# GpSimd makes the first guesses of the reciprocal roots from block 2 on, and blocks 0 and 1 are started tile by tile with ScalarE's square roots

## The chip, the cores and the metric

The kernel runs on one core of one Trainium2 chip. The metric is the device time of that core in microseconds. Three runs of the kernel before took 392.67, 393.62 and 393.69 us; their median is 393.62 us.

## What is computed

The input x has 2 sequences of 4096 tokens with 256 features. Each token is layer-normalised; the result xn goes into two branches, and both are added to x.

```python
xn = (x - mean(x)) / sqrt(var(x) + 1e-5)
# branch 1: causal softmax pooling
h   = tanh(xn @ W1 + b1)                    # 256 -> 256
s   = h @ w2 + b2                           # one score a token
e   = exp(s - max over the sequence of s)
ctx = cumsum(e * xn) / cumsum(e)            # along the sequence
a   = tanh(concat(ctx, xn) @ Wc.T + bc)     # 512 -> 256
# branch 2: gated feed-forward, integer weights times 1/127
f   = (silu(xn @ wg.T) * (xn @ wu.T)) @ wd.T   # 256 -> 768 -> 256
out = x + a + f
```

## The kernel before

**Tiling.** The 8192 tokens are cut into 16 blocks of 512, a block into two pairs of 256 tokens, a pair into two tiles of 128. Matmuls take fp16 operands in two parts, a high part and the rest, so that one product is two or three passes. All sums are made in the 8 PSUM banks.

**Order.** The kernel is written as steps with a short name, a block and an index. Each engine's order is worked out while the program is built: `due_times()` gives every step a due time, `STEP` its engine, how long it keeps it and when its result is seen, `needs()` what it waits for, and the class `Plan` lets each engine take, at each modelled moment, the first step in order of due time that is ready and, if it opens a PSUM bank, finds one free. `SENT` and `X_SENT` are the modelled landings of the weights and of the first blocks of x. On the chip each engine then runs its own list in order and waits on semaphores.

**Steps around the change** (lines of the kernel before):

- `stats_first`, `root_first`, `normalise_first` (L958 to L1033), on VectorE, for block 0: statistics of four tiles, variance plus eps (L1014), ScalarE's square root (L1368), reciprocal and one Newton step, then four normalised tiles (L1031), signalled in pairs.
- Ahead of that TensorE runs `WARM` = 12 matmuls on constants (L1381), spreads the bias row b1 and the row w2 over the partitions by matmuls with ones (L1377), and runs twice `FILL` = 2 more matmuls on constants.
- `Lb` (L700): transposes of a normalised pair; `Xh` (L873, ScalarE) and `Xl` (L1091, VectorE): high part and rest of xn out of the bank. Only blocks 0 and 1 are turned like this; from block 2 on a pair is turned by transposing DMAs (`Tx`), after `Xh` (L869) and `Xm` (GpSimd, L1244).
- `W1h` (L917, ScalarE) and `W1l` (L1144, VectorE): the parts of W1. `Ea` (L912, ScalarE) copies the spread rows out of the last bank. `Ss` (L841, ScalarE) writes b1 into a bank before `S` (L707, TensorE) adds xn @ W1 to it; `Th` (L882, ScalarE) is its tanh, in place, and `Sv` (L1101, VectorE) the product with w2 and its sum. The bank is free after `Sv`.
- `Gg`, `Gu` (L743, TensorE, four 512-column matmuls each, 6 of either a block), `Sg` (L888, ScalarE, silu), `H` (L1116), `Hh` (L895), `Hl` (L1121), then `D` (L763, TensorE). `C` (L707 too) is the product with Wc.
- `Tb` (L914): ScalarE's load of the table with tanh and silu, after block 0's square root.
- `B` (L951, L955, VectorE): statistics of a pair. `R` (`root_seed`, L971, VectorE, four operations): first guess of the reciprocal root by an integer shift. `T` (`root_newton`, L985, GpSimd): three Newton steps and the shift, 14 small operations for a group of one or two blocks. `Ln` (L859, ScalarE) or `Lp` (L1239, GpSimd) normalises. `STAT_GROUPS` has ten groups; groups 1 to 9 go through `R` and `T`.
- `Wgh`, `Wuh`, `Wdh` (GpSimd, L1249, L1252, L1255): integer weights to fp16. `N` (L1225, L1230) and `Cl` (L1258): GpSimd's part of the context sums.
- The bank of an `Lb` is freed by `Xl`, and `S` of block 0 runs pair by pair.

Of the kernel before, what the change touches and what calls it, by code (L numbers as in the profile page):

```python
# [16 lines left out]
P = 128  # L17
# [10 lines left out]
EPS = 1e-5  # L28
# [16 lines left out]

STAT_GROUPS = [[0], [1], [2], [3], [4, 5], [6, 7], [8, 9], [10, 11], [12, 13], [14, 15]]
# [19 lines left out]
    "T": (PO, 1.35, 1.45), "N": (PO, 3.2, 3.3), "Cl": (PO, 1.2, 1.3), "Lp": (PO, 0.75, 0.85), "Xm": (PO, 1.5, 1.6),  # L66
# [3 lines left out]
    "Ea": (SE, 0.5, 0.63), "Tb": (SE, 1.4, 1.5), "W1h": (SE, 0.55, 0.7), "Wch": (SE, 1.06, 1.2), "Kx": (SE, 1.02, 1.2), "Ky": (SE, 1.02, 1.2),  # L70
    "W1l": (VE, 0.62, 0.75), "Wcl": (VE, 1.2, 1.3), "K1": (VE, 0.62, 0.75), "Kg": (VE, 0.9, 1.0), "Kh": (VE, 0.9, 1.0), "Ku": (VE, 0.5, 0.6), "Kd": (VE, 0.5, 0.6), "Ke": (VE, 0.5, 0.6),
    "Kc": (VE, 1.2, 1.3), "Kf": (VE, 0.75, 0.85), "Fl": (VE, 0.15, 0.25),
    "Wgh": (PO, 1.5, 1.6), "Wuh": (PO, 1.5, 1.6), "Wdh": (PO, 1.5, 1.6), "Kp": (TE, 0.15, 0.4),
# [3 lines left out]
OPENS = {"Kp": "Kp", "Lb": "Lb", "Ss": "S", "Gg": "Gg", "Gu": "Gu", "Cs": "C", "M1": "M1", "M2": "M2", "M3": "M3"}  # L77
CLOSES = {"Kp": "Fl", "Lb": "Xl", "S": "Sv", "Gg": "Sg", "Gu": "Hl", "D": "Da", "M1": "V1", "M2": "V2", "M3": "V3"}
# [55 lines left out]
def closing(group):  # L134
    kind, i, x = group
    if kind == "C":
        return ("Ct" if seeded(i, x) else "Ca"), i, x
    return CLOSES[kind], i, x


def closed_by(st):
    kind, i, x = st
    if kind in ("Ct", "Ca"):
        return ("C", i, x) if closing(("C", i, x)) == st else None
    for group, last in CLOSES.items():
        if last == kind:
            return group, i, x
    return None


def due_times():
# [26 lines left out]
    for g, blocks in enumerate(STAT_GROUPS):  # L178
        if g:
# [7 lines left out]
            due["R", g, 0] = root  # L187
            for n in range(NEWTON):
                due["T", g, n] = root + 0.1 + 1.4 * n
    for i in range(NBLK):  # L190
        for pr in range(2):
# [8 lines left out]
            due["Ss", i, pr] = due["S", i, pr] - (1.6 if i or not pr else 0.6)  # L200
            due["Th", i, pr], due["Sv", i, pr] = end["S", i, pr] + 0.1, end["S", i, pr] + 0.8
# [36 lines left out]
def needs(st, wide):  # L238
# [3 lines left out]
    if kind in ("W1h", "Wgh", "Ea"):  # L242
        return []
# [1207 lines left out]
```

## Time and profile before

| | us |
|---|---|
| runs of the kernel before | 392.67, 393.62, 393.69 |
| the profiled execution, its own time | 393.06 |
| its span on the core | 391.1 |
| TensorE busy in it | 385.9 |
| VectorE, ScalarE, GpSimd busy | 297.5, 235.6, 210.1 |

The span is what the views of the trace cover; 1.96 us of the execution lie around it. A start is in microseconds from the start of the span. PE is TensorE, PEld its weight loads, DVE VectorE, ACT ScalarE, POOL GpSimd, SP SyncE; L707 is line 707 of the kernel. A matmul's row gives when it starts and how long it takes through the array; matmuls are pipelined, so the distance of their starts is what they cost.

### The profile page before, as it was taken

The numbers are of one execution on the slowest core, as the hardware profiler recorded it, in microseconds if no ns is written. First come the engines' busy times: TensorE is split into PE (matmuls) and PEld (weight loads), VectorE is DVE, ScalarE is ACT, GpSimd is POOL, SyncE is SP. The second block draws the span as 40 slices with busy tenths as digits, with TensorE's granted clock in tenths as the row PEclk, the third lists the DMA queues.
The fourth block names the chain that finished last, engine by engine and source line by source line (L and its number), as shares of the span: only waits on it lengthen the run. The fifth ranks groups of instructions, "written<-read, shape, count | busy, mean of one in ns | idle before, by whom it ended". The sixth has DMA issues, their size and how long they took to land.

```text
span 391.1 us, 7885 instructions
## 1 busy us (share of the span) xinstructions
PE 385.9 (99%) x2740; PEld 268.7 (69%) x2740; DVE 297.5 (76%) x632; ACT 235.6 (60%) x434; POOL 210.1 (54%) x289
## 2 busy tenths in 40 slices
PE   8999999999999999999999999999999999999996
PEld 4556676757566686866877676767677676676765
DVE  6799998999996997876769966777676765754351
ACT  4766576689985659786556575364553644536250
POOL 1487586874629989794335405866456554502000
PEclk9999999999999999999999999999999999999999
DMA  8944525576834232475210005043231220100001
GB/s 275 348 158 69 137 53 134 106 189 89 201 72 96 54 83 81 116 165 97 76 34 29 27 28 164 28 128 87 58 72 55 90 85 26 54 28 28 28 28 61
DMA packets 54945, 36.56 MB, mean 93 GB/s; under 512 B 31858, under 2 KB 50292, under 8 KB 54900
## 3 DMA queue, kind: packets, MB, share of 16 engines
q1 hardware_dynamic: 54608, 35.73, 35.5%
q8 instruction: 24, 0.39, 0.4%
q10 hardware_dynamic: 292, 0.26, 0.2%
q14 instruction: 21, 0.17, 0.1%
HBM read 20.19 MB, written 8.45 MB: 73 GB/s over the span
## 4 chain that ended last, share of the span: by engine, by line
PE 97%; DVE 2%; issue 0%; DVEq 0%
PE bank L707 44%; PE bank L743 41%; PE bank L763 9%; PE bank L1381 1%; DVE ex L1121 0%; DVE stats L951 0%; PE bank L700 0%; PE bank L1377 0%; DVE veps L980 0%; DVE xt L1091 0%; DVE bank L1116 0%; DVE sg L1413 0%; PE bank L813 0%; DVE mv L955 0%; PE bank L819 0%
## 5 line engine op out<-in xcount | busy, mean ns | idle before, releaser
L743 PE MATMUL bank<-xt,narrow 128*128 128x512 f16 x768 | 177.3, 379 | 0.0
L743 PEld LDWEIGHTS bank<-xt,narrow 128*128 128x128 f16 x768 | 75.2, 98 | 75.4 <-DVE wide L1121 0.2
L707 PE MATMUL bank<-narrow,wide 128*128 128x256 f16 x792 | 96.4, 273 | 0.0
L707 PE MATMUL bank<-narrow,xt 128*128 128x256 f16 x768 | 92.8, 273 | 0.3 <-DVE xt L1091 0.3
L707 PEld LDWEIGHTS bank<-narrow,xt 128*128 128x128 f16 x768 | 75.0, 98 | 19.0 <-DVE xt L1091 0.6
L1258 POOL TENSOR_TENSOR wide<-ex,wide 128x512 f16<-128x512 f32 x32 | 39.4, 1248 | 87.6 <-ACT wide L909 87.6
L888 ACT ACTIVATE sg<-bank 128x512 f32<-128x512 f32 x96 | 57.2, 596 | 46.3 <-PE bank L743 45.6
L1116 DVE SCALAR_TENSOR_TENSOR bank<-bank,sg 128x512 f32<-128x512 f32 x96 | 66.1, 694 | 24.4 <-PE bank L743 21.3
L707 PEld LDWEIGHTS bank<-narrow,wide 128*128 128x128 f16 x792 | 77.5, 98 | 9.4
L895 ACT ACTIVATE wide<-bank 128x512 f16<-128x512 f32 x90 | 53.3, 596 | 47.7 <-DVE bank L1116 39.3
L1121 DVE TENSOR_TENSOR wide<-bank,wide 128x512 f16<-128x512 f32 x90 | 60.5, 678 | 9.9 <-ACT wide L895 8.6
L1139 DVE TENSOR_TENSOR_SCAN ex<-rows,ex 128x512 f32<-128x512 f32 x32 | 56.5, 1767 | 0.7 <-POOL ex L1230 0.7
L1230 POOL TENSOR_TENSOR ex<-ex,rows 128x512 f32<-128x512 f32 x32 | 44.8, 1401 | 9.2 <-DMA rows<-scratch 6.9
L1225 POOL TENSOR_TENSOR ex<-xt 128x512 f32<-128x512 f16 x32 | 44.6, 1395 | 0.2
L1125 DVE TENSOR_TENSOR xres<-bank,xres 128x512 f32<-128x512 f32 (+1 forms) x33 | 22.0, 667 | 26.4 <-PE bank L707 26.3
L841 ACT ACTIVATE bank<-every 128x512 f32<-128x512 f32 (+1 forms) x65 | 38.3, 594 | 0.0
L763 PE MATMUL bank<-narrow,wide 128*128 128x256 f16 x312 | 38.3, 273 | 0.0
L902 ACT ACTIVATE bank<-bank 128x512 f32<-128x512 f32 (+1 forms) x33 | 18.8, 569 | 31.0 <-PE bank L707 31.0
L763 PEld LDWEIGHTS bank<-narrow,wide 128*128 128x128 f16 x312 | 30.5, 98 | 7.4
L1130 DVE TENSOR_TENSOR xres<-bank,xres 128x512 f32<-128x512 f32 x28 | 19.3, 688 | 18.2 <-ACT bank L902 18.1
L1101 DVE CUSTOM_DVE_ANT_0 bank<-bank,every 128x256 f32<-128x256 f32 x64 | 25.4, 446 | 4.1 <-ACT bank L882 4.1
L1244 POOL TENSOR_TENSOR xt<-xnat,xt 128x512 f16<-128x512 f32 x14 | 16.9, 1226 | 11.3 <-ACT xt L869 11.3
(103 smaller groups left out, 262.3 us busy)
## 6 DMA issues: line engine op xcount, KB each, us to landing
rows<-scratch SPq DMA_DIRECT2D x16, 512.0 KB, 5.1
out_y<-xres SPq DMA_DIRECT2D x31, 256.0 KB, 2.1
xres<-in_x SPq DMA_DIRECT2D x15, 512.0 KB, 5.1
xt<-xt SPq DMA_TRANSPOSE x56, 2.5
wide<-in_wg SPq DMA_DIRECT2D x1, 768.0 KB, 5.9
wide<-in_wu SPq DMA_DIRECT2D x1, 768.0 KB, 8.4
wide<-in_wd SPq DMA_DIRECT2D x1, 768.0 KB, 10.1
wide<-in_wc SPq DMA_DIRECT2D x1, 512.0 KB, 11.1
```

Source lines behind the costliest of these rows:

```text
L707: return pe.matmul(dst, lhs, rhs, start=False, stop=stop, skip_group_check=True)
L743: mm = pe.matmul(b[:, :], pg.up(which, k, j), pg.xn(sx, k, tok), start=n == 0, stop=n == len(todo) - 1)
L763: mm = pe.matmul(dst, lhs, rhs, start=n == 0, stop=n == len(todo) - 1)
L841: act.activation(b[:, 0:n * D].rearrange("p (t d) -> p t d", t=n), row.to_broadcast([P, n, D]), ACT.Copy, scale=pg.sum_up).then_inc(done, 1)
L888: act.activation(sg[:, m % SG_RING, :], bank_of(pg, "Gg", i, n)[:, :], ACT.Silu, scale=pg.silu_scale).then_inc(a_sg, 1)
L895: act.activation(pg.h(0, m, slice(0, BLK)), bank_of(pg, "Gu", i, n)[:, :], ACT.Copy).then_inc(a_h, 1)
L1116: dve.scalar_tensor_tensor(out=dst, in0=b[:, :], scalar=pg.up_scale, in1=sg[:, m % SG_RING, :], op0=ALU.mult, op1=ALU.mult).then_inc(v_h, 1)
L1121: dve.tensor_tensor(pg.h(1, m, slice(0, BLK)), bank_of(pg, "Gu", i, n)[:, :], pg.h(0, m, slice(0, BLK)), ALU.subtract).then_inc(v_hlo, 1)
L1139: dve.tensor_tensor_scan(t, rows[:, i % 2, 1, :], t, 0.0 if first else ex[:, (i - 1) % EX_RING, n, BLK - 1:BLK], ALU.mult, ALU.add).then_i ...
L1225: pool.tensor_tensor(dst, xt16[:, 0, k, tok], xt16[:, 1, k, tok], ALU.add).then_inc(g_x, 1)
L1230: pool.tensor_tensor(dst, src, rows[:, i % 2, 0, :], ALU.mult).then_inc(g_ex, 1)
L1258: pool.tensor_tensor(pg.ctx(1, i, k, slice(0, BLK)), ex[:, i % EX_RING, k, :], pg.ctx(0, i, k, slice(0, BLK)), ALU.subtract).then_inc(g_cl ...
```

## The change

1. `ROOTS` = 2: groups 0 and 1 get their roots as group 0 did, with ScalarE's square root (`square_root`, now straight from the variance with eps as a bias) and one Newton step on VectorE. Block 1 so has no `T` on GpSimd; its square root (`Rq`) stands ahead of the table load `Tb`. From group 2 on the first guess is a GpSimd step `Sd` of three operations in place of VectorE's four (`R`).
2. Block 0 is handled by tiles: `L0`, `X0`, `Y0` in place of `Lb`, `Xh`, `Xl`, with a semaphore for each tile, and `first_scores` orders block 0's score matmuls as the tiles come.
3. The rows: `Ea` and the row of w2 on TensorE are gone. `Ss` of block 0 reads b1 from the bank into which TensorE spread it; b1 for later blocks and w2 come by DMAs of SyncE's queue (`b1_every` ahead of wd, `w2b` ahead of Wc).
4. The tanh of blocks 0 and 1 (`AWAY` = 2) is written to the tile `rows`, so that the bank is free after `Th`, and their `Sv` is due 25 modelled us later.
5. `WARM` is 9 and `FILL` 4, at one place. `Wgh` and `Wuh` are made in halves. Modelled times are changed.

```diff
+AWAY = 2
+ROOTS = 2
+WARM, FILL = 9, 4
-BEGIN = {TE: 7.3, SE: 5.7, VE: 8.1, PO: 1.0, SY: 12.0}
+BEGIN = {TE: 6.9, SE: 5.6, VE: 7.8, PO: 1.0, SY: 12.0}
...
     if kind == "Tb":
-        return [(("Xh", 0, 1), 0)]
+        return [(("X0", 0, 3), 0), *((("Rq", g, 0), 0) for g in range(1, ROOTS))]
+    if kind == "Rq":
+        return [(("B", i, 1), 0)]
...
+        def turn_tile(pe, t):
+            pe.wait_ge(v_xn, t + 1)
+            for k in range(KD):
+                mm = pe.transpose(bank_of(fits, "L0", 0, t)[:, k * P:(k + 1) * P], xnat[:, t // 2, t % 2, k * P:(k + 1) * P], ident[:, :])
+            mm.then_inc(p_x0, 1)
+
+        def first_scores(pe, pr):
...
+            if not pr:
+                pe.wait_ge(a_w, 1)
+                for t in range(4):
+                    pe.wait_ge(a_ss, t // 2 + 1)
+                    pe.wait_ge(a_x0, t + 1)
+                    onto(t, 0, 0)
+                pe.wait_ge(v_w, 1)
+                for t in range(4):
+                    onto(t, 0, 1)
+            for t in (2 * pr, 2 * pr + 1):
+                pe.wait_ge(v_x0, t + 1)
+                mm = onto(t, 1, 0, True)
+            mm.then_inc(p_s, 1)
...
+        def square_root(act, g):
+            act.wait_ge(v_mv, 2 * g + 2)
+            act.activation(rstd[:, columns(g)], mv[:, columns(g), 1], ACT.Sqrt, bias=eps[:, 0:1]).then_inc(a_root, 1)
...
             elif kind == "Ss":
-                act.wait_ge(a_b, 1)
                 act.wait_ge(p_warm, 1)
-                bias_seed(act, pg, 0, open_bank(act, pg, "S", i, n), a_ss)
+                if i or pg.wide:
+                    act.wait_ge(s_b1, 16)
+                    bias_seed(act, pg, 0, open_bank(act, pg, "S", i, n), a_ss)
+                else:
+                    act.wait_ge(p_b, 1)
+                    spread_row(act, pg, bank[ROW_BANK][:, 0:D], open_bank(act, pg, "S", i, n), a_ss)
...
-                act.activation(b[:, :], b[:, :], ACT.Tanh, scale=1.0 / pg.sum_up).then_inc(a_s, 1)
+                act.activation(rows[:, i, n, :] if i < AWAY else b[:, :], b[:, :], ACT.Tanh, scale=1.0 / pg.sum_up).then_inc(a_s, 1)
...
+            elif kind == "X0":
+                act.wait_ge(p_x0, n + 1)
+                act.activation(xt16[:, 0, :, n * P:(n + 1) * P], half(bank_of(pg, "L0", 0, n)[:, 0:D]), ACT.Copy,
+                               scale=X_UP).then_inc(a_x0, 1)
...
-            step(dve.tensor_scalar(veps[:, t], mv[:, t, 1], EPS, None, ALU.add))
-            dve.tensor_scalar(minus_half[:, t], veps[:, t], -0.5, None, ALU.mult)
-            step(dve.tensor_scalar(seed[:, t], veps[:, t].bitcast(I32), 1, None, ALU.logical_shift_right))
-            step(dve.tensor_scalar(rstd[:, t].bitcast(I32), seed[:, t], -1.0, MAGIC, ALU.mult, ALU.add))
+            pool.wait_ge(v_mv, 2 * STAT_GROUPS[g][-1] + 2)
+            step(pool.tensor_scalar(veps[:, t], mv[:, t, 1], 1.0, EPS, ALU.mult, ALU.add))
+            pool.tensor_scalar(minus_half[:, t], veps[:, t], -0.5, 0.0, ALU.mult, ALU.add)
+            step(pool.tensor_scalar(rstd[:, t].bitcast(I32), veps[:, t].bitcast(I32), -0.5, MAGIC, ALU.mult, ALU.add))
...
-            step(dve.tensor_scalar(veps[:, t], mv[:, t, 1], EPS, None, ALU.add))
-            dve.tensor_scalar(minus_half[:, t], veps[:, t], -0.5, None, ALU.mult)
-            dve.wait_ge(a_root, 1)
+            dve.wait_ge(v_mv, 2 * g + 2)
+            dve.tensor_scalar(minus_half[:, t], mv[:, t, 1], EPS, -0.5, ALU.add, ALU.mult)
+            dve.wait_ge(a_root, g + 1)
...
             sp.dma_start(half(wu32.bitcast(I32)), rows_of(wu)).then_inc(s_wu, 16)
+            sp.dma_start(b1_every, biases[0:D].partition_broadcast(P)).then_inc(s_b1, 16)
             sp.dma_start(wd32.bitcast(I32).rearrange("p (k n) -> p k n", k=KH), rows_of(wd)).then_inc(s_wd, 16)
             load_x(sp, 2)
+            sp.dma_start(w2b, w2b2_in[0:D].partition_broadcast(P)).then_inc(s_w2, 16)
...
-            act.dma_start(w2_row, w2b2_in[0:D].rearrange("(o d) -> o d", o=1)).then_inc(s_w2, 16)
...
-            to_every(bank[BANKS - 1], 0, b_row)
-            to_every(bank[BANKS - 1], D, w2_row).then_inc(p_b, 1)
+            pe.matmul(bank[ROW_BANK][:, 0:D], ones[0:1, :], b_row, start=True, stop=True).then_inc(p_b, 1)
```

## Rows read from the trace of the kernel before

**Rows 1.** The page: busy time and share by engine, and the chain by engine.
```profile
PE 385.9 (99%) x2740; PEld 268.7 (69%) x2740; DVE 297.5 (76%) x632; ACT 235.6 (60%) x434; POOL 210.1 (54%) x289
...
PE 97%; DVE 2%; issue 0%; DVEq 0%
```

**Rows 2.** Busy time by windows, PE alone: window, its length, busy (instructions), clock, DMA, GB/s.
```profile
1.50:5.40 3.90, 3.88 (x10) 1.00 0.93 267
...
9.10:11.70 2.60, 2.60 (x25) 1.00 1.05 380
11.70:21.20 9.50, 9.50 (x46) 1.00 1.10 345
21.20:24.60 3.40, 3.06 (x22) 1.00 0.86 270
24.60:388.00 363.40, 363.14 (x2624) 1.00 0.32 79
```

**Rows 3.** Timeline, PE: start, us, engine, line, operation, how many, idle before.
```profile
6.11 1.13 PE L1377 MATMUL bank<-sg,ones 1*128 1x256 f32 x4
...
9.12 2.78 PE L707 MATMUL bank<-narrow,xt 128*128 128x256 f16 x24
11.74 9.66 PE L743 MATMUL bank<-xt,narrow 128*128 128x512 f16 x44
...
23.17 1.04 PE L707 MATMUL bank<-narrow,xt 128*128 128x256 f16 x8
24.54 1.92 PE L707 MATMUL bank<-narrow,xt 128*128 128x256 f16 x16 [0.33 <-DVE xt L1091]
```

**Rows 4.** Timeline, ACT, 5 to 17 us.
```profile
6.43 0.63 ACT L917 ACTIVATE narrow<-wide 128x512 f16<-128x512 f32 x1 [0.60 <-DMA wide<-in_w]
7.28 0.60 ACT L912 ACTIVATE every<-bank 128x512 f32<-128x512 f32 x1 [0.22 <-PE bank L1377]
7.90 0.60 ACT L841 ACTIVATE bank<-every 128x512 f32<-128x512 f32 x1
8.44 1.07 ACT L873 ACTIVATE xt<-bank 128x512 f16<-128x512 f32 x2
...
10.02 1.28 ACT L914 ACT_TABLE_LOAD   x1
```

**Rows 5.** Timeline, DVE lines, 0 to 26 us.
```profile
5.42 0.17 DVE L1014 TENSOR_SCALAR veps<-mv 128x4 f32<-128x4 f32 x1
...
6.74 1.38 DVE L1031 TENSOR_SCALAR xnat<-xres,mv,rstd 128x256 f32<-128x256 f32 x4
...
10.26 0.74 DVE L951 BATCH_NORM_STATS2 stats<-xres 128x6 f32<-128x256 f32 x2
...
22.43 0.85 DVE L980 TENSOR_SCALAR veps<-mv 128x4 f32<-128x4 f32 x1
```

**Rows 6.** Timeline, POOL, 20 to 30 us.
```profile
21.78 1.47 POOL L1255 TENSOR_SCALAR narrow<-wide 128x1536 f16<-128x1536 int32 x1
23.84 0.20 POOL L995 TENSOR_TENSOR newton<-rstd 128x4 f32<-128x4 f32 x1 [0.58 <-DVE rstd L983]
24.12 0.20 POOL L996 TENSOR_TENSOR newton<-newton,minus_half 128x4 f32<-128x4 f32 x1
```

**Rows 7.** DMA queues from 4.2 to 6 us: packets, MB, share of 16 engines.
```profile
q1 hardware_dynamic: 354, 0.53, 99.7%
```

**Rows 8.** Instructions of L902 and L859: duration ns min/median/max, first and last start.
```profile
L902 ACT ACTIVATE bank<-bank x33: 368/582/592, 142.7 to 382.5; 128x512 f32<-128x512 f32 x31, 128x256 f32<-128x256 f32 x2
...
L859 ACT ACTIVATE xt<-xres,shift,rstd x16: 585/592/601, 80.2 to 169.5; 128x256 f32<-128x256 f32 x16
```

**Rows 9.** Windows: DVE alone from 80 us, then POOL alone from 120 and 150 us.
```profile
80.00:100.00 20.00, 19.39 (x62) 1.00 0.75 167
...
120.00:130.00 10.00, 9.77 (x8) 1.00 0.15 30
150.00:160.00 10.00, 9.84 (x8) 1.00 0.19 45
```

More of the change, by code:

```diff
@@ L137, in closing @@
         return ("Ct" if seeded(i, x) else "Ca"), i, x
+    if kind == "S" and i < AWAY:
+        return "Th", i, x
     return CLOSES[kind], i, x
@@ L186, in due_times @@
             root = first - (8.5 if FIRST_T in blocks else 8.5)
-            due["R", g, 0] = root
-            for n in range(NEWTON):
+            due["R" if g < ROOTS else "Sd", g, 0] = root
+            if g < ROOTS:
+                due["Rq", g, 0] = root
+            for n in range(NEWTON * (g >= ROOTS)):
                 due["T", g, n] = root + 0.1 + 1.4 * n
@@ L362, in __init__ @@
         self.place, self.before, self.held = {}, {}, dict.fromkeys(range(BANKS))
-        self.whole = {n: not wide and n < BANKS - 1 for n in range(BANKS)}
-        self.open_now, self.freed = set(), {n: 9.0 if n == BANKS - 1 else 0.0 for n in range(BANKS)}
+        self.whole = {n: not wide and n != ROW_BANK for n in range(BANKS)}
+        self.open_now, self.freed = set(), {n: 7.6 if n == ROW_BANK else 0.0 for n in range(BANKS)}
         self.behind, self.freed_behind = set(), set()
@@ L442, in start @@
         _, busy, seen = STEP[st[0]]
+        if st[:2] == ("S", 0) and not self.wide:
+            busy, seen = (0.44, 0.68) if st[2] else (2.18, 2.42)
         if st[0] in ("C", "D") and len(tiles_of(*st[1:])) == 1:
@@ L686, in open_bank @@
                 eng.wait_ge(*pg.freed(last))
-            elif pg.plan.place[kind, i, n] == BANKS - 1:
-                eng.wait_ge(a_b, 1)
+            elif pg.plan.place[kind, i, n] == ROW_BANK and not pg.wide:
+                eng.wait_ge(a_ss, 2)
             return bank_of(pg, kind, i, n)
@@ L789, in tensor_step @@
                 turn(pe, pg, i, n)
+            elif kind == "L0":
+                open_bank(pe, pg, kind, i, n)
+                turn_tile(pe, n)
+            elif kind == "S" and (i or pg.wide):
+                scores(i, n)
             elif kind == "S":
-                scores(i, n)
+                first_scores(pe, n)
             elif kind in ("Gg", "Gu"):
@@ L1375, in _ @@
             pe.wait_ge(v_set, 2)
-            def to_every(b, at, row):
-                return pe.matmul(b[:, at:at + row.shape[1]], ones[0:1, :], row, start=at == 0, stop=True,
-                                 skip_group_check=True)
             def warm_up(n):
@@ L1387, in _ @@
             pe.wait_ge(s_b, 16)
-            pe.wait_ge(s_w2, 16)
-            to_every(bank[BANKS - 1], 0, b_row)
-            to_every(bank[BANKS - 1], D, w2_row).then_inc(p_b, 1)
-            spare_bank = next(FITS.place["Gg", 0, j] for j in range(KH) if FITS.before["Gg", 0, j] is None and FITS.place["Gg", 0, j] < BANKS - 1)
+            pe.matmul(bank[ROW_BANK][:, 0:D], ones[0:1, :], b_row, start=True, stop=True).then_inc(p_b, 1)
             for n in range(FILL):
-                warm_up(spare_bank)
+                warm_up(FITS.place["L0", 0, 0])
             pe.wait_ge(s_ident, 16)
@@ L1415, in _ @@
             stats_first(dve)
-            root_first(dve)
-            for pr in range(2):
-                normalise_first(dve, pr)
+            root_first(dve, 0)
+            for c in range(4):
+                normalise_first(dve, c)
             for kind, i, n in FITS.early(VE):
```

231 lines of the change are left out of this document (132 added, 99 removed).

## The prediction

> **What bounds the kernel now.** I read the page first. TensorE is busy for 385.9 of 391.1 us and holds 97% of the chain that ended last, VectorE 2% [rows 1]. So the second view was TensorE alone by windows [rows 2]. From 24.6 us to the end of its work it is busy for 363.14 of 363.40 us with 2624 instructions; from 11.7 to 21.2 us it is busy throughout. It has no wait to give back in either. What it computes there is the same before and after. The time can therefore move in three places only: the moment at which the dense stream begins (the first `Gg` at 11.74 us [rows 3]), the one visible hole (3.06 busy of 3.40 us between 21.2 and 24.6 us [rows 2]), and holes that a new order might open.
>
> The hole is a wait of block 1's scores for VectorE's `Xl`. Eight score matmuls start at 23.17, the sixteen others at 24.54 [rows 3]. Sixteen cost 1.92 - 0.17 = 1.75 us by starts, 0.109 each, so the eighth starts at 23.17 + 7 x 0.109 = 23.93 and the ninth could at 24.04: 0.50 us lost. The window's 0.34 is smaller since it counts the drain of the array as busy. From 21.2 to 24.54, 3.34 us, TensorE starts block 1's eight transposes, four 512-column matmuls of `Gg` or `Gu` and the eight of the scores: 8 x 0.109 + 4 x 0.216 + 8 x 0.109 = 2.61 us (0.109 for a transpose is an estimate). So 0.7 us is lost in all, 0.5 of it in front of `Xl`.
>
> VectorE was late with `Xl` because block 2's first guess stood ahead of it: its first operation, on 4 elements, took 0.85 us, where the same operation of block 0 took 0.17 [rows 5]. It ran from 22.43 to 23.28, and GpSimd's conversion of wd ran from 21.78 to 23.25 [rows 6]. The small VectorE operation ended just when GpSimd's long one did, in this trace.
>
> **The start, step by step.** Before, ScalarE makes the parts of W1 at 6.43 (when W1 has landed), copies the spread rows at 7.28 (after TensorE's rows), seeds the first bank at 7.90, evicts the two pairs from 8.44, and TensorE's 24 score matmuls begin at 9.12 [rows 3, 4]. 24 x 0.109 = 2.62 gives 11.74.
>
> *Rows.* After, nine matmuls on constants replace twelve. Before, ten took 3.88 us, 0.43 us apart, which is TensorE's 1.2 GHz level (the 512-column matmuls of `Gg` cost 9.50/44 = 0.216 us, the 2.4 GHz level) [rows 2]. So nine end near 1.5 + 9 x 0.43 = 5.4 us. The bias row has landed: from 4.2 us on all 354 packets are of SyncE's queue and none of ScalarE's [rows 7]. One row is half of L1377's four instructions, 0.57 of 1.13 us [rows 3], and some 0.2 of latency, so b1 is spread at 6.2 to 6.5 us. This is before W1 is dealt with (7.06), so it costs and gives nothing.
>
> *Roots.* `veps` (0.17, with its signal 0.21) leaves the chain [rows 5]. The square root now has a pointer as bias. An activation on 256 columns without pointers takes 0.368 us, one with scale and bias pointers 0.592 [rows 8], so one pointer costs some 0.11. The chain gains 0.1 us; the four normalised tiles come from 6.64 to 8.02 instead of 6.74 to 8.12.
> By the Trainium skill (ScalarE: Activation LUTs, What ACT_TABLE_LOAD costs) each [128,1] pointer operand adds about 93 ns. The rows agree, and by the page's figure the chain would gain 0.12.
>
> *ScalarE.* This engine sets the new start. W1 6.43 to 7.06; two seeds at the distance of 7.90 to 8.44, 0.54 each, until 8.14; four tiles, 0.37 us each [rows 8] and 0.31 apart with the same overlap of 0.06: the last one ends at 8.14 + 0.93 + 0.37 = 9.44. The transposes are not later: tile by tile after 8.02 they end by 8.5, while `X0` of tile 3 starts at 9.07. After the fourth tile, with the 0.09 from eviction to matmul seen before, TensorE still has 2 + 8 + 8 = 18 score matmuls, 1.96 us: the first `Gg` starts at 9.53 + 1.96 = 11.49, 0.25 us earlier than 11.74. VectorE's rests (`Y0`, one 0.4 us behind each `X0`) come by 9.9, and the matmuls that need them start after 10.6. Bounds: if W1 lands earlier, the transposes set the pace; last tile transposed 8.5, evicted 8.97, `Gg` at 11.0 (-0.7 us). If W1 or the row comes late by 0.4, `Gg` is 0.15 late. I take -0.3: the row's value and a little of the earlier side, as one small DMA leaves ScalarE's queue. The removed fillers between transposes and scores covered a wait and cost nothing.
>
> **Block 1.** It no longer waits for 14 GpSimd operations at 0.28 us (23.84 to 24.12 [rows 6]), 3.9 us. Instead: its statistics, which began at 10.26 [rows 5]; two pairs at 1.0 us, 12.3; square root 0.3; five small VectorE operations of 0.2, 13.6; `Lp` two pairs of 1.1 us, 15.9 behind the second weight conversion. `Lb` can then stand at 16 instead of 21.2 us, with block 0's `Gg`/`Gu` around it. VectorE also loses before 24 us: block 1's old guess, block 2's guess with its 0.85, and block 0's `Sv` (moved on by 25 us). It gains R and a little for the halves of `Y0`, about 1.2. So `Xl` is in time and the 0.7 us go. Bounds: 0 (another step is late in its place) to -0.7. I take -0.6.
>
> **From block 2 on.** GpSimd takes three operations for each of eight groups, 8 x 3 x 0.28 = 6.7 us, less the 3.9 of block 1. VectorE loses four each, at least 0.7 a group. TensorE waited for neither after 24.6 us [rows 2], so this is worth 0, though VectorE is busy for 19.39 of 20 us at 80 us, and GpSimd for 9.77 and 9.84 of 10 at 120 and 150 us [rows 9]. The `Sv` of blocks 0 and 1, eight operations on 256 elements of some 0.4 us (estimate: two tiles' statistics take 0.74 [rows 5]), fall into VectorE's full stretch; what it lost pays for them. The DMA queue gets two spread rows of 128 KB, at 345 GB/s [rows 2] 0.4 us each: b1's lands after wu, near 12.5, and is needed for block 1's seeds, some 2 us later; wd and x behind it have more. I put 0 for all this, -0.1 to +1.5.
>
> **Sum.** -0.3 - 0.6 + 0 = -0.9 us. Against the profiled execution (393.06 = 391.1 + 1.96) that is 392.2; against the median 393.62 it is 392.7. The profiled execution lies between the three runs, so I take 392.4. Its own range is 391.6 to 393.4. A measurement here can tell about 0.3%, 1.18 us, so the border of faster is 392.44 and the forecast lies on it.
>
> **Rivals.**
> *Only the start moves.* The hole is not closed but moved: some other VectorE step (`H`, the `Xl` itself) is late since VectorE is full anyhow. For: it is busy 97% at 80 us [rows 9]. Against: it loses 2 to 3 us of work before 24 us. 393.6 - 0.3, or 393.06 - 0.3: about 393.0.
> *W1 earlier.* It was ScalarE's only DMA wait, 0.60 us [rows 4]. With W1 at 6.0, -0.7 and -0.6: 391.9.
> *The first guesses do nothing.* This is inside the forecast: without them the sum is the same but for the 0.85 us operation.
> *Slower: the banks are held by the later table load.* `Tb` must follow block 1's square root. Table load 1.28 (10.02 before [rows 4]), now from 12.6; tanh from 14.1, silu from 15.2 instead of 12.8. TensorE starts at 11.45, and with two banks held by block 0's scores has six for `Gg`/`Gu`: six x 0.864 = 5.2 us, until 16.6. The first tanh ends at 14.7. Each us by which x of block 1 is later than 12.3 (it was there at 10.26) is a us of idle TensorE; ScalarE and VectorE, 3 us behind, could make it 2 us. With the start and hole gains: 393.3 - 0.9 + 2 = 394.4. Against: two us of margin.
> *Slower: the clock rises late.* Nine matmuls end at 5.4, just where the pace went from 0.43 to 0.216. If it stays at 1.2 GHz, four fillers cost 0.84 more, 24 score matmuls 2.6: less what waits cover, 395.3. Against: in the trace before it had risen by the tenth matmul, after 3.9 us of dense work, and that stretch is the same.
> By the Trainium skill (TensorE: Matmul & The Clock Gate, Part 1) the array starts at half rate and the moment of release isn't tied to the kernel's start, so it differs between executions; no row of one execution shows that.
>
> **How the numbers follow.** Forecast 0.58, only the start 0.13, W1 earlier 0.12, banks or another step of the new order 0.09, clock 0.08. Faster: half of the forecast and W1 earlier, 0.42. Same: 0.28 + 0.13 = 0.41. Slower: 0.17. The range 391.5 to 394.2 leaves out the clock and part of the banks and of the lower end.
>
> **What the profile will show.** Right: `Gg` first at 11.3 to 11.6; ScalarE from W1 to the fourth `X0` without a wait; `Lb` of block 1 near 16 us; no window of TensorE between 12 and 380 us under 99%. Wrong: `Gg` at 11.7 or later (the start), a TensorE wait for VectorE before 30 us (the hole), for ScalarE's `Sg` or `Th` near 16.6 (banks), for GpSimd's `Cl` after 120 us (guesses), or a pace of 0.43 after 5.5 us (clock).

## The result and the profile after

The changed kernel takes 396.54 us (median of 8 runs, 394.81 to 397.23); the kernel before takes 393.37 us (8 runs, 392.67 to 393.97). The ratio is 1.0073, with a 95% interval of 1.0051 to 1.0094: 3.2 us slower. Forecast were 392.4 us and a range of 391.5 to 394.2; the result lies outside.

The eight times of the changed kernel stand in two groups: 394.81, 394.90, 395.05, and 396.25 to 397.23. The mean granted clock of an execution, 1.000 for full speed, separates them too: 0.999 to 1.000 in the three, 0.994 to 0.996 in the five. The profiled execution took 397.23 us with a span of 395.1 and a mean clock of 0.994, so it is of the upper group.

TensorE alone by windows of the changed kernel (columns as in [rows 2]):

```profile
16.70:19.60 2.90, 2.79 (x16) 1.00 1.12 335
19.60:22.20 2.60, 0.00 (x0) 0.95 1.10 348
22.20:24.80 2.60, 2.58 (x13) 0.50 1.09 354
24.80:27.80 3.00, 3.00 (x15) 0.91 0.40 131
...
30.00:380.00 350.00, 350.00 (x2510) 1.00 0.33 81
```

Everything is lost before 30 us. There is a stretch of 2.6 us without one matmul, and behind it one with a granted clock of 0.50, which is the 1.2 GHz level. From 30 to 380 us TensorE is busy all the time, as before [rows 2]. The timeline of TensorE:

```profile
8.30 2.42 PE L761 MATMUL bank<-narrow,xt 128*128 128x256 f16 x20
10.83 1.02 PE L814 MATMUL bank<-xt,narrow 128*128 128x512 f16 x4
11.69 0.60 PE L761 MATMUL bank<-narrow,xt 128*128 128x256 f16 x4
...
18.54 1.03 PE L814 MATMUL bank<-xt,narrow 128*128 128x512 f16 x4
22.22 2.74 PE L782 MATMUL bank<-narrow,xt 128*128 128x256 f16 x12 [2.65 <-ACT bank L920]
24.75 3.04 PE L814 MATMUL bank<-xt,narrow 128*128 128x512 f16 x12
27.63 1.47 PE L782 MATMUL bank<-narrow,xt 128*128 128x256 f16 x12
```

Four terms can be read off, against [rows 3]:

- The start. The first `Gg` is at 10.83 instead of 11.74, but four of block 0's score matmuls (0.44 us) come behind it. That is 0.47 us gained.
- The hole in front of block 1's scores. The last four-matmul product (`Gg` or `Gu`) before it has its last matmul at 18.54 + 3 x 0.216 = 19.19, and the next could start at 19.41; the scores start at 22.22. 2.81 us lost.
- The clock behind the hole. Twelve 256-column matmuls take 24.75 - 22.22 = 2.53 us instead of 1.31, and the next twelve of 512 columns 2.88 instead of 2.59. 1.5 us lost.
- The old hole of 0.7 us is gone; some 0.4 us of small gaps are there instead, among them 0.34 in front of block 1's transposes.

-0.47 + 2.81 + 1.51 - 0.7 + 0.37 = 3.5 us, and the last matmul of the kernel does start that much later (the row of its last 54 matmuls, products with Wc, starts at 385.19 instead of 381.68). The span is 4.0 us longer. The other 0.5 us lie behind VectorE's last operation, where the last outputs go out: 3.8 us instead of 3.3. In the profiled executions of the first three experiments this end takes 3.4 to 3.9 us, so it is not put down to the change.

Who held TensorE back? The waits up to 60 us (engine and line that waited, for whom, us in total, times, longest):

```profile
ACT ex L982 <- DVE bank L1209: 3.0, 1, 3.0
PE bank L782 <- ACT bank L920: 2.6, 1, 2.6
DVE rows L1194 <- DMA every<-in_w2b: 2.3, 1, 2.3
```

Read from the last line upwards this is one chain, and the timelines of the three engines show it in order:

```profile
14.87 1.07 ACT L969 ACTIVATE rows<-bank 128x512 f32<-128x512 f32 x2
15.82 1.57 ACT L975 ACTIVATE sg<-bank 128x512 f32<-128x512 f32 x3
...
17.70 0.43 DVE L1194 CUSTOM_DVE_ANT_0 rows<-rows,every 128x256 f32<-128x256 f32 x1 [2.34 <-DMA every<-in_w2b]
...
17.79 1.67 POOL L1351 TENSOR_SCALAR narrow<-wide 128x1536 f16<-128x1536 int32 x1
...
18.05 1.68 DVE L1194 CUSTOM_DVE_ANT_0 rows<-rows,every 128x256 f32<-128x256 f32 x1
20.35 1.29 DVE L1209 SCALAR_TENSOR_TENSOR bank<-bank,sg 128x512 f32<-128x512 f32 x2
...
21.07 0.60 ACT L982 ACTIVATE ex<-bank 128x512 f16<-128x512 f32 x1 [3.03 <-DVE bank L1209]
21.57 0.60 ACT L920 ACTIVATE bank<-every 128x512 f32<-128x512 f32 x1
```

The last two lines are ScalarE's again. The first `Sv` (L1194) waits until 17.70 us for the spread row w2, which SyncE's queue brings behind the third load of x. Its second operation takes 1.68 us instead of 0.4. Behind the four of them stand the `H` (L1209), from 20.35 instead of the 16.35 of the kernel before. ScalarE waits in `Hh` (L982) for the first `H`, and the seed of block 1's scores (L920) stands behind that `Hh`. TensorE waits for the seed.

### The profile page after: what moved, and what is told of

Read it like the earlier page. It is cut to its first block, busy times and chain, and to the rows that moved or that the text cites. A ratio compares the mean times of both kernels' runs of the same rounds, so it can differ in the third digit from the quotient of the medians.

```text
span 395.1 us, 7867 instructions
## 1 busy us (share of the span) xinstructions
PE 386.6 (98%) x2735; PEld 268.6 (68%) x2735; DVE 290.5 (74%) x604; ACT 234.2 (59%) x436; POOL 213.6 (54%) x301
## 4 chain that ended last, share of the span: by engine, by line
PE 94%; DMA 2%; DVE 1%; issue 1%; SPq 1%; ACT 0%; POOL 0%; POOLq 0%; DVEq 0%
PE bank L782 43%; PE bank L814 40%; PE bank L834 9%; DMA xres<-in_x 2%; DVE stats L1041 0%; DVE minus_half L1103 0%; SPq L1372 0%; DVE newton L1106 0%; DVE rows L1194 0%; PE bank L746 0%; DVE bank L1209 0%; ACT bank L920 0%; POOL xnat L1335 0%; SPq L1439 0%; PE bank L889 0%
## 5 line engine op out<-in xcount | busy, mean ns | idle before, releaser
L814 PE MATMUL bank<-xt,narrow 128*128 128x512 f16 x768 | 178.4, 379 | 0.1
L814 PEld LDWEIGHTS bank<-xt,narrow 128*128 128x128 f16 x768 | 75.3, 98 | 75.0 <-issue 0.6
L782 PE MATMUL bank<-narrow,xt 128*128 128x256 f16 x744 | 91.5, 275 | 2.6 <-ACT bank L920 2.6
L1209 DVE SCALAR_TENSOR_TENSOR bank<-bank,sg 128x512 f32<-128x512 f32 x96 | 66.2, 696 | 29.9 <-PE bank L814 23.7
L782 PEld LDWEIGHTS bank<-narrow,xt 128*128 128x128 f16 x744 | 73.3, 99 | 21.8 <-ACT bank L920 3.1
L975 ACT ACTIVATE sg<-bank 128x512 f32<-128x512 f32 x96 | 56.9, 596 | 52.6 <-PE bank L814 51.1
L982 ACT ACTIVATE wide<-bank 128x512 f16<-128x512 f32 x90 | 53.2, 594 | 43.7 <-DVE bank L1209 37.5
L1232 DVE TENSOR_TENSOR_SCAN ex<-rows,ex 128x512 f32<-128x512 f32 x32 | 53.8, 1681 | 0.4 <-POOL ex L1326 0.4
L1326 POOL TENSOR_TENSOR ex<-ex,rows 128x512 f32<-128x512 f32 x32 | 46.1, 1442 | 8.6 <-DMA rows<-scratch 6.3
L920 ACT ACTIVATE bank<-every 128x512 f32<-128x512 f32 (+1 forms) x63 | 37.1, 592 | 0.0
L1340 POOL TENSOR_TENSOR xt<-xnat,xt 128x512 f16<-128x512 f32 x14 | 16.1, 1159 | 16.8 <-ACT xt L952 16.8
L1194 DVE CUSTOM_DVE_ANT_0 bank<-bank,every 128x256 f32<-128x256 f32 x56 | 22.4, 443 | 2.4 <-ACT bank L969 2.4
```

What stands on the lines that cost most here:

```text
L782: return pe.matmul(dst, lhs, rhs, start=False, stop=stop, skip_group_check=True)
L814: mm = pe.matmul(b[:, :], pg.up(which, k, j), pg.xn(sx, k, tok), start=n == 0, stop=n == len(todo) - 1)
L920: act.activation(b[:, 0:n * D].rearrange("p (t d) -> p t d", t=n), row.to_broadcast([P, n, D]), ACT.Copy, scale=pg.sum_up).then_inc(done, 1)
L975: act.activation(sg[:, m % SG_RING, :], bank_of(pg, "Gg", i, n)[:, :], ACT.Silu, scale=pg.silu_scale).then_inc(a_sg, 1)
L982: act.activation(pg.h(0, m, slice(0, BLK)), bank_of(pg, "Gu", i, n)[:, :], ACT.Copy).then_inc(a_h, 1)
L1209: dve.scalar_tensor_tensor(out=dst, in0=b[:, :], scalar=pg.up_scale, in1=sg[:, m % SG_RING, :], op0=ALU.mult, op1=ALU.mult).then_inc(v_h, 1)
```

## The experiments

The kernel before ran beside every experiment. Its median was 393.48 us beside the first four, 393.40 beside the four with twelve and two, with nine and two, with w2 behind wu and with the guesses back, and 393.61 beside the last three. Each ratio is to those runs. Where an experiment's executions stand in two groups, the higher one is called the upper group.

### w2 ahead of wu

```diff
+            sp.dma_start(w2b, w2b2_in[0:D].partition_broadcast(P)).then_inc(s_w2, 16)
             sp.dma_start(half(wu32.bitcast(I32)), rows_of(wu)).then_inc(s_wu, 16)
...
             load_x(sp, 2)
-            sp.dma_start(w2b, w2b2_in[0:D].partition_broadcast(P)).then_inc(s_w2, 16)
```

> The changed kernel with one DMA moved: the spread row w2 is issued ahead of wu instead of behind the third load of x. In the changed kernel VectorE stood from 15.36 to 17.70 us at the first Sv for it, and TensorE had a hole of 2.8 us at 19.4. Theory (the wait for w2 holds VectorE, whose H comes late, so that ScalarE's seed of block 1 comes late): that wait is gone, the hole is under 0.8 us, the clock stays up, 391.8 to 392.8 us. Rival A (the hole comes of the later table load and of VectorE meeting GpSimd's long conversions, whatever w2 does): the hole stays at 2 us or more, 395 us or more. Rival B (the guesses on GpSimd cost): as A, with the loss after 30 us.

Measured: 393.66 us (10 runs, 392.28 to 394.38), ratio to before 1.0002 (0.9988 to 1.0016). The wait for w2 and the hole of 2.8 us are gone, the clock stays at 1.00 there, and 2.9 us of the 3.2 are given back. The time is still above the 391.8 to 392.8 that were expected. TensorE's timeline in the same stretch:

```profile
14.73 1.89 PE L814 MATMUL bank<-xt,narrow 128*128 128x512 f16 x8 [0.17 <-POOL narrow L1348]
17.45 0.63 PE L746 MATMUL bank<-ident,xnat 128*128 128x128 f32 x4 [0.84 <-POOL xnat L1335]
...
20.08 1.47 PE L782 MATMUL bank<-narrow,xt 128*128 128x256 f16 x12
```

Two smaller holes are left (0.33 and 1.0 us by starts), so the expected 0.8 at most was missed: wu is later behind w2, and GpSimd's `Lp` (L1335) is late. Against rival A, that the late table load makes the hole, this run says little, since its table load came at 12.45, an us earlier than the 13.46 of the changed kernel. Twelve and two, below, settles it.

### The scores later

```diff
-        self.times = {0.0, *BEGIN.values(), *SENT.values(), *X_SENT}
+        self.times = {0.0, 30.0, *BEGIN.values(), *SENT.values(), *X_SENT}
...
         t = X_SENT[st[1]] if st[0] == "B" and st[1] < FIRST_X else SENT.get(st[0], 0.0)
+        if st[0] == "Sv" and st[1] < AWAY and not self.wide:
+            t = 30.0
```

> The changed kernel with its DMAs as they are; in the planner the Sv of blocks 0 and 1 are not ready before 30 modelled us, so VectorE's order has the H and Xl first. Theory: H is no longer behind the wait for w2, the hole is under 0.5 us, 391.6 to 392.6 us, a little under the kernel with w2 early since VectorE also has 1.7 us less to do before block 1's Xl. Rival A: the hole stays (the late table load gives silu at 15.8 as before), 395 us. Rival B: 396.

Measured: 392.29 us (7 runs: 392.05 to 392.72, and one of 393.65), ratio 0.9967 (0.9956 to 0.9979). With the DMAs as the change has them and only VectorE's order altered, the changed kernel is 1.2 us faster than the kernel before. So it takes both, an operand that lands late and the `Sv` in front of the `H`: the run before took away the first, this one the second, and the hole went in either. The `Sv` in front of the `H` alone do not make it (see w2 behind wu). The profiled execution was the one of 393.65 us, and its TensorE rows showed something new:

```profile
1.55 4.02 PE L1475 MATMUL bank<-sg 128*128 128x512 f16 x9 [1.55 <-DVE sg L1502]
5.50 1.22 PE L1482 MATMUL bank<-sg,ones 1*128 1x256 f32 x2
6.65 1.89 PE L1475 MATMUL bank<-sg 128*128 128x512 f16 x4
8.33 1.92 PE L755 MATMUL bank<-ident,xnat 128*128 128x128 f32 x8
...
12.41 1.03 PE L816 MATMUL bank<-xt,narrow 128*128 128x512 f16 x4
```

The four matmuls on constants at 6.65 take 0.43 us each, the pace of 1.2 GHz. The eight transposes behind them are (10.04 - 8.33)/8 = 0.214 us apart, where the four at 18.02 are 0.11 apart, so the slow pace lasted until after 10 us. `Gg` comes at 12.41 instead of 10.83. After that there is no hole at all. So a slow start of its own exists, worth 1.6 us.

### The hole filled

```diff
             for kind, i, n in FITS.early(TE):
+                if (kind, i, n) == ("S", 1, 0):
+                    pe.wait_ge(*fits.freed(("Gg", 0, 2)))
+                    for _ in range(9):
+                        mm = pe.matmul(bank_of(fits, "S", 1, 0)[:, :], fits.up(0, 0, 0), fits.xn(0, 0, slice(0, BLK)), start=True, stop=True)
+                    mm.then_inc(p_fill, 1)
                 tensor_step(pe, fits, kind, i, n)
```

ScalarE's seed of block 1 (`Ss`) waits for these nine as well.

> The changed kernel with nine 512-column matmuls on old data between the last Gu before the hole and block 1's first scores, into the bank that the seed will get; the seed waits for them. They take 1.9 us of a hole of 2.8. Theory of the clock (idling 2.8 us lets TensorE fall to 1.2 GHz, which costs 1.3 to 1.5 us by the 12 score matmuls at 0.213 instead of 0.109 and two more): no fall in any execution, the times stand together at 394.8 to 395.3 us, where those of the changed kernel lay between 394.81 and 397.23. Rival (the clock falls by itself or for another cause): 396.5 with the same spread.

Measured: 395.17 us (5 runs: 394.76, 395.14, 395.17, 395.45, and 396.60), ratio 1.0048 (1.0030 to 1.0066).

```profile
18.90 2.10 PE L1492 MATMUL bank<-xt,narrow 128*128 128x512 f16 x9
21.74 1.49 PE L783 MATMUL bank<-narrow,xt 128*128 128x256 f16 x12 [0.74 <-ACT bank L921]
23.07 2.75 PE L815 MATMUL bank<-xt,narrow 128*128 128x512 f16 x12
```

Twelve score matmuls now take 1.33 us, not 2.53. The work behind the hole is still late, 21.74 us, 0.6 of it since the seed waits for the nine, but it is not slower. Four of five runs lie where the lower three of the changed kernel's eight lie, and none of the five has a mean clock under 0.999. Nor has any of the 27 executions of the three kernels with nine and four and the scores later one under 0.998. So the 0.994 to 0.996 of the changed kernel's upper five point to a clock that fell in the hole, as it did in the profiled one. Why it did not fall in the other three is not shown, since none of them was profiled. They may be executions with the slow start of the run before: the end of the hole hangs on the landing of w2, so a start 1.6 us later would leave a hole of 1.2 us (an estimate, 2.8 - 1.6). The fifth run here, 396.60, was not profiled either; it is as far above the others as the slow start costs.

### Both edits

Its diff is those of the first two experiments.

> Both edits: w2 ahead of wu, and the Sv of blocks 0 and 1 not before 30 modelled us. Theory: as with the Sv later alone, 391.6 to 392.6 us; no wait for w2 was left to remove, so the two are the same within 0.3 us. If it were faster by more, the waits for w2 at the later place would still cost. Rival A: 395 us.

Measured: 393.31 us (8 runs: 392.20, 392.29, 392.40, 393.12, and 393.49 to 394.29), ratio 0.9987 (0.9972 to 1.0002). The lower group is where that of the scores later is. The median is not, since five of eight are above 393; the profiled one (393.80) has the slow start again, with four matmuls on constants in 1.9 us and the first `Gg` at 12.34, and no hole. The expectation, 391.6 to 392.6, was missed, as far as this one profile tells because of the start, which no theory had yet.

### Twelve and two matmuls on constants

```diff
-WARM, FILL = 9, 4
+WARM, FILL = 12, 2
```

on top of the scores later.

> The kernel with the Sv later, and at the start twelve matmuls on constants instead of nine and two instead of four behind the bias row (as many as before). In the profiled execution of the kernel with the Sv later the pace stayed at 0.427 us until 8.3 us and Gg came first at 12.41; in the one with w2 early it rose near 5.3 and Gg came at 10.51. Theory W (nine leave the rise of the clock to chance, twelve don't): Gg at 11.0 to 11.3 in the profile, all executions within 1 us, median 392.2 to 392.7. Rival P (how late the clock rises depends on when the execution starts and not on the number): the same two groups near 392.2 and 393.7, in like shares.

Measured: 392.33 us (12 runs: nine from 391.77 to 392.46, three from 392.98 to 393.27), ratio 0.9976 (0.9967 to 0.9986). The upper group is still there, but it is smaller and 0.8 us away instead of 1.6. Theory W is half right: the number does not abolish it. The median is in its range, but not all executions are within 1 us.

```profile
1.55 4.27 PE L1475 MATMUL bank<-sg 128*128 128x512 f16 x12 [1.55 <-DVE sg L1502]
...
7.13 1.38 PE L755 MATMUL bank<-ident,xnat 128*128 128x128 f32 x8 [0.15 <-DVE xnat L1122]
8.35 2.42 PE L763 MATMUL bank<-narrow,xt 128*128 128x256 f16 x20
10.60 1.03 PE L816 MATMUL bank<-xt,narrow 128*128 128x512 f16 x4
```

Three more matmuls on constants cost nothing when the clock is up: the transposes wait for VectorE's first tile anyway. This kernel is 1.1 us under the kernel before, with an interval clear of it, and 4.2 under the changed one. Its median is that of the scores later (392.29, seven runs); which of the two is faster can't be told.

This run also settles rival A of the first experiments. It has the fast start (`Gg` at 10.60), and ScalarE's tanh and silu are as late as in the changed kernel (14.87 and 15.82):

```profile
13.28 1.28 ACT L1006 ACT_TABLE_LOAD   x1
...
14.68 1.07 ACT L971 ACTIVATE rows<-bank 128x512 f32<-128x512 f32 x2
15.64 1.58 ACT L977 ACTIVATE sg<-bank 128x512 f32<-128x512 f32 x3
```

TensorE's one gap between 11 and 30 us is 0.35 us by starts, in front of block 1's transposes at 16.57. So the late table load does not make the hole.

### Nine and two

```diff
-WARM, FILL = 9, 4
+WARM, FILL = 9, 2
```

on top of the scores later.

> The kernel with the Sv later, nine matmuls on constants, and two instead of four behind the bias row. When the pace is still 0.427 us there, the four last until 8.3 us and hold the first transposes, which could run from 7.0 on. Theory: in executions with the late clock it gives back 0.7 to 0.9 us (393.7 becomes 392.9), in the others nothing, so that the median is 392.2 to 392.8 and the spread under 1 us. Rival: the idling that it leaves makes the clock rise late more often, median 393.5 or more.

Measured: 393.38 us (12 runs: four from 392.12 to 392.36, eight from 393.35 to 394.63), ratio 0.9997 (0.9983 to 1.0010). Expected were 392.2 to 392.8; the median is nearer to the rival's 393.5. A gain in the late case exists (the profiled one has `Gg` at 11.86, not 12.41: 0.55 us, where 0.7 to 0.9 stood), but eight of twelve are now in the upper group, where it was ten of 27 in the three kernels with nine and four and the scores later (that one, both edits, and the guesses back). The counts are small; that fewer matmuls make it likelier is what they point to, no more. Three of the eight (393.89 to 394.63) have a mean clock of 0.994, the others 1.000.

### The kernel before with nine

```diff
-        WARM, FILL = 12, 2
+        WARM, FILL = 9, 2
```

> The kernel before with nine matmuls on constants ahead of the bias row instead of twelve, nothing else changed. Theory W (the number decides how often the clock rises late): its times fall into two groups as those of the changed kernels do, near 392.6 and 394.3, and its median is 0.1 to 1 us above that of the kernel before. Rival P (the number does not matter, only the moment at which the execution starts): the distribution of the kernel before, median within 0.3 us or up to 0.5 us faster.

Measured: 393.25 us (12 runs: seven from 392.91 to 393.26, five from 394.39 to 395.95), ratio 1.0007 (0.9990 to 1.0024). The kernel before, in 29 runs beside it, lay between 392.98 and 394.33 without a gap. The better executions are some 0.5 us under its median of 393.61, the others 0.8 to 2.3 us above it. The two groups are what theory W expected, but the median is not: it is 0.4 us under that of the kernel before, where W had it above, and that is rival P's range. So the number of matmuls does change the distribution, and it is not shown to change the median for the worse. In the profiled one (394.39) the clock had risen and fell again:

```profile
6.30 0.60 PE L1381 MATMUL bank<-sg 128*128 128x512 f16 x2
7.61 1.53 PE L700 MATMUL bank<-ident,xnat 128*128 128x128 f32 x8 [0.70 <-DVE xnat L1031]
8.93 1.06 PE L1381 MATMUL bank<-sg 128*128 128x512 f16 x2
9.79 3.76 PE L707 MATMUL bank<-narrow,xt 128*128 128x256 f16 x24
```

Two constant matmuls take 0.60 us at 6.30 and 1.06 at 8.93, and from 9 to 10 us the granted clock reads 0.50. Between them are an idle 0.70 us and eight transposes.

### w2 behind wu, and the tanh in the bank

```diff
             sp.dma_start(half(wu32.bitcast(I32)), rows_of(wu)).then_inc(s_wu, 16)
+            sp.dma_start(w2b, w2b2_in[0:D].partition_broadcast(P)).then_inc(s_w2, 16)
             sp.dma_start(b1_every, biases[0:D].partition_broadcast(P)).then_inc(s_b1, 16)
...
             load_x(sp, 2)
-            sp.dma_start(w2b, w2b2_in[0:D].partition_broadcast(P)).then_inc(s_w2, 16)
```

This is the changed kernel with one DMA moved; its `Sv` stand where the change has them.

> The changed kernel with w2's DMA right behind wu and ahead of b1's, and the Sv where the planner of the change puts them. In the kernel with w2 ahead of wu VectorE's wait for w2 was gone but TensorE lost 1.3 us of its own: 0.3 us since wu was late, 1.0 us ahead of block 1's transposes. Theory: w2 lands by 14.5 us, before the first tanh ends, so no wait for it; wu is not later; the hole is under 1.0 us; 392.2 to 393.9 by the clock's two groups. Rival A (VectorE's 1.7 us of Sv in front of H are enough for the hole): hole of 1.5 us or more, 394 or more.

Measured: 393.37 us (10 runs, 392.13 to 394.27), ratio 1.0001 (0.9988 to 1.0014). No wait for w2, wu not late, and no hole in front of block 1's scores, so rival A (the work of the `Sv` in front of the `H` is enough for it) falls. The hole in front of block 1's transposes stays: the last matmul before them starts at 16.06, the next could at 16.28, and they start at 17.27, 1.0 us. It was to be under 1.0 and isn't. So one more edit, on top of this one:

```diff
-AWAY = 2
+AWAY = 0
```

> The kernel with w2 behind wu and its Sv where the change puts them, but the tanh of blocks 0 and 1 stays in the PSUM bank (AWAY 0), so that Sv has one operand in PSUM instead of two in SBUF. In the kernel with w2 behind wu GpSimd's four normalisations of block 1 took 3.10 us while VectorE ran four Sv beside them, 2.17 us in the kernel whose Sv came later, and TensorE stood 1.0 us in front of block 1's transposes. Theory C (VectorE's operations with two SBUF operands and GpSimd shut each other out): the four take 2.2 us although the Sv run beside them, the hole is under 0.4 us, about 0.7 us faster. Rival (they are slow for another cause, such as the loads in the DMA queues): 3.0 us and the hole of 1.0 stay.

GpSimd's four normalisations of block 1, in the kernel with w2 behind wu, in the kernel with twelve and two (no `Sv` beside them), and in this one:

```profile
15.10 3.10 POOL L1335 TENSOR_SCALAR xnat<-xres,rstd,shift 128x256 f32<-128x256 f32 x4 [0.78 <-DVE shift L1111]
```

```profile
15.33 2.17 POOL L1337 TENSOR_SCALAR xnat<-xres,rstd,shift 128x256 f32<-128x256 f32 x4 [0.78 <-DVE shift L1113]
```

```profile
15.47 2.18 POOL L1335 TENSOR_SCALAR xnat<-xres,rstd,shift 128x256 f32<-128x256 f32 x4 [0.77 <-DVE shift L1111]
...
15.56 0.43 DVE L1194 CUSTOM_DVE_ANT_0 bank<-bank,every 128x256 f32<-128x256 f32 x1 [0.27 <-ACT bank L969]
```

In the third the `Sv` run beside them from 15.56 to 17.2 us, and they take 2.18 us. Theory C holds: with both operands in SBUF, where the program's tiles lie, `Sv` costs GpSimd 0.9 us here, and beside GpSimd's conversion of 1.67 us one `Sv` operation takes 1.3 us longer in the changed kernel. With one operand in PSUM neither happens. The second half of that stands in the trace of the kernel before, whose tanh stays in the bank: its conversion of wu runs beside the `Sv`, and both keep their usual lengths.

```profile
12.11 1.48 POOL L1252 TENSOR_SCALAR narrow<-wide 128x1536 f16<-128x1536 int32 x1 [1.97 <-DMA wide<-in_wu]
```

```profile
12.49 0.47 DVE L1101 CUSTOM_DVE_ANT_0 bank<-bank,every 128x256 f32<-128x256 f32 x1
```
By the Trainium skill (GPSIMD Engine Reference, Key points) GpSimd shares its SBUF interfaces with VectorE and contends with instructions that have two SBUF inputs; these rows agree, 3.10 against 2.18.
The time, 393.69 us (10 runs: 392.83 to 393.10 and 394.29 to 394.88), ratio 1.0003 (0.9989 to 1.0017), did not fall by the expected 0.7; the median is 0.3 higher than with the tanh in SBUF. The better group lies above the two fastest executions of that kernel (392.13 and 392.35) and under its profiled one (393.24, with the fast start), so the groups don't tell which way it moved. The profile has a hole of 0.64 us at 106 us, where TensorE waits for a silu (`L814 <- ACT sg L975: 0.5`) that this kernel's new order puts late. Whether the hole in front of block 1's transposes went cannot be said: its profiled execution had the slow start, and there the hole is covered.

### The first guesses back on VectorE

```diff
-    "Sd": (PO, 0.85, 0.95)
+    "Sd": (VE, 0.84, 0.94)
...
-            step(pool.tensor_scalar(veps[:, t], mv[:, t, 1], 1.0, EPS, ALU.mult, ALU.add))
-            pool.tensor_scalar(minus_half[:, t], veps[:, t], -0.5, 0.0, ALU.mult, ALU.add)
-            step(pool.tensor_scalar(rstd[:, t].bitcast(I32), veps[:, t].bitcast(I32), -0.5, MAGIC, ALU.mult, ALU.add))
+            step(dve.tensor_scalar(veps[:, t], mv[:, t, 1], EPS, None, ALU.add))
+            dve.tensor_scalar(minus_half[:, t], veps[:, t], -0.5, None, ALU.mult)
+            step(dve.tensor_scalar(seed[:, t], veps[:, t].bitcast(I32), 1, None, ALU.logical_shift_right))
+            step(dve.tensor_scalar(rstd[:, t].bitcast(I32), seed[:, t], -1.0, MAGIC, ALU.mult, ALU.add))
```

on top of the scores later with nine and four:

> The kernel with the Sv later, and the first guesses from block 2 on made by VectorE in four operations as before. It undoes the part that the change is named after. Theory: TensorE waited for neither engine after 30 us in the changed kernel, so nothing moves: within 0.4 us of the kernel with the Sv later in the better group of executions (392.1 to 392.5), and no idle stretch of TensorE after 30 us. Rival B (the guesses on GpSimd cost): 1 us or more faster. The other side (they were a gain): VectorE late at its Xl again and a hole at 22 to 25 us, 392.7 to 393.2.

and with twelve and two:

> The kernel with the Sv later and twelve and two matmuls on constants, and in addition the first guesses back on VectorE in four operations. Against the same kernel with the guesses on GpSimd (392.33 us) it gives their worth without the two groups of the start. Theory: nothing, 392.1 to 392.6. Other side: VectorE late in front of block 1 or 2, 392.9 or more; GpSimd late, 391.9 or less.

Measured: 392.49 us (12 runs: eight from 391.91 to 392.94, four from 393.55 to 394.12), ratio 0.9990 (0.9977 to 1.0003), against 0.9967 (0.9956 to 0.9979) with the guesses on GpSimd; and 393.08 us (12 runs: five from 392.03 to 392.87, seven from 393.04 to 393.74), ratio 0.9984 (0.9975 to 0.9994), against 0.9976 (0.9967 to 0.9986). The first is inside its expected range. The second is not: 392.1 to 392.6 were expected, and 393.08 lies on the side that was named for VectorE being late, 0.75 us above the same kernel with the guesses on GpSimd. The lower groups agree within 0.15 us at their middles; what differs is how many executions are in the upper one, four and seven of twelve against one of seven and three of twelve. Both profiles have one small wait that the others lack:

```profile
PE bank L837 <- DVE ex L1220: 0.2, 1, 0.2
```

It is some 0.4 us by starts, in front of block 0's down projection. The hole of the kernel before, in front of block 1's scores, does not come back. So what the profiles show for the guesses on GpSimd is a worth of 0 to 0.4 us, and rival B falls. The rest of the 0.75 us lies in the upper group: the profiled execution with twelve and two (393.21) has all twelve matmuls at the slow pace and its `Gg` at 11.80 instead of 10.60. That the upper group's share depends on the guesses is not shown and has no reason in the traces, as the guesses come after it is decided.

## Why the prediction was wrong, point by point

**The start was right in kind and a little small.** -0.3 was forecast, -0.47 measured. W1 was there at 5.95 instead of 6.43 (the rival "W1 earlier"), and ScalarE's chain followed without a wait, as the steps had it: seeds at 6.49, first tile at 7.53. `Gg` at 10.83 where 11.3 to 11.6 stood.

**Block 1 early was right.** Its transposes start at 16.78 us where 16 was forecast, 21.2 before. The old hole is gone. The 0.8 us were lost at a place that the prediction had just read in the kernel before: a small VectorE operation that meets a long GpSimd one. Two of the five small operations of block 1's root took 0.84 and 0.68 us beside the conversion of wu (13.13 to 14.76), not 0.2. And moving block 2's guess was not what closed the old hole: with the guesses back on VectorE it stays closed.

**The step that failed is the one on the DMA queue and on `Sv`.** The prediction costed the two spread rows by their bytes, said who waits for b1's, and said of the rest that "wd and x behind it have more". It did not ask who waits for w2's: the first `Sv`. And it took the 25 us by which the `Sv` are due later for a time at which they run. A due time only ranks what is ready. VectorE had nothing else ready before the first silu, so the planner gave it both `Sv` of block 0 at 14.7 modelled us, ahead of the `H`, and its model knows no landing for w2. "Block 0's `Sv` moved on by 25 us" was counted as relief for VectorE; it was in fact the wait of 2.34 us and 2.65 us of work (17.70 to 20.35) in front of the step that ScalarE needed. The prediction put 0 for the queue and the `Sv` together; the trace has the hole of 2.81 us there. Moving only the `Sv` gave 392.29 us, 0.1 from the forecast. Moving only the row gave 2.9 of the 3.2 us back.

**The rival with the banks had the place and not the cause.** It put the danger at 16.6 us with tanh and silu 3 us late. They were that late (14.87 and 15.82), and by themselves cost nothing: with the `Sv` out of the way they are as late (14.68 and 15.64, twelve and two), and TensorE has no such hole.

**The rival with the clock had too small a chance and too high a price.** "That stretch is the same" was the argument against it, from one execution. It isn't the same each time: with nine and four and the scores later, ten of 27 executions are in the upper group, and the two of them that were profiled had the late rise. It costs 1.6 us by the first `Gg`, where the rival had 2.9 above the forecast. By the Trainium skill (TensorE: Matmul & The Clock Gate, Part 1) the moment of release is not tied to the kernel's start and varies between executions. The runs agree: behind the same nine matmuls it came near 5 us or only after 10. But this is not what made the changed kernel slow; its profiled execution had the early rise.

**A second term was missing, the clock in a hole.** The sum had nothing for what idle time does to TensorE's clock. The 2.8 us without a matmul cost 1.5 more in the profiled execution, and the mean clocks point to five such executions of eight.

**The range.** It left out the wait for w2 and the fall of the clock behind it, 2.81 and 1.51 us. Less the gains they make the 3.5 us of the profiled execution. No rival stood for either of the two.

**From block 2 on** nothing was forecast for the guesses, and nothing beyond 0.4 us was found.

**Open.** How much of the upper groups is a late rise and how much a fall after a rise. Both were seen in profiled executions. In the column that gives the clock a late rise reads 1.00 (scores later, 8.3 to 10 us: 1.00 at half the pace), so an unprofiled execution with a mean clock of 0.994 to 0.996 had a fall: three of eight with nine and two, two of five in the kernel before with nine. The rest is not known. In the changed kernel wg and block 1's x were used later than before (statistics of block 1 from 11.16, after a wait of 1.3 us, against 10.26 [rows 5]). In the kernel with the hole filled, whose DMAs are the same, they began at 9.89, so this differs from execution to execution.

## What to carry to other kernels

When a change brings an operand by another queue, list every instruction that waits for it and what stands behind that instruction on its engine, before counting bytes: 128 KB of w2 were an estimated 0.4 us of bandwidth and cost TensorE 4.3 us. In a list order worked out by due times, postponing a step means making it not ready; a later due time alone lets an idle engine take it first. And a warm-up or a hole on TensorE has to be judged over many executions, since the clock turns one into a gain and another into a loss.

## What the runs showed of the hardware

- A hole of 2.8 us in TensorE's stream let its granted clock fall to 0.50 in the profiled execution, and the mean clocks (0.994 to 0.996) point to the same in five of eight; with nine matmuls in the hole it stayed at 1.00.
- The page prints a clock of 1.00 for the first microseconds, while 512-column matmuls are 0.427 us apart there. The pace of the matmuls shows the level, the column does not.
- Among kernels that begin with the same nine matmuls at 1.55 us, the pace had risen by 6.5 us at the latest in five profiled executions (the four matmuls on constants behind the bias row take 1.04 us). In four others it rose only after 10 us (the four take 1.89 us, or two of them 1.03, and the eight transposes behind them 1.71 by starts).
- VectorE's product of two SBUF tiles and GpSimd's normalisation slow each other (3.10 against 2.18 us for four operations); with one operand in PSUM they don't (2.18). One such product took 1.68 us beside a conversion of 1.67, and 0.47 beside one of 1.48 when an operand lay in PSUM.
